# Relative-value picks as transposes in the PSUM ring, and VectorE's lower-part subtraction behind its casts

## The reference

```python
scores = jnp.einsum('bhld,bhrd->bhlr', Q, K) * scale
scores = scores + jnp.einsum('bhld,lrd->bhlr', Q, rel_k)
attn = jax.nn.softmax(scores, axis=-1)
out = jnp.einsum('bhlr,bhrd->bhld', attn, V)
out = out + jnp.einsum('bhlr,lrd->bhld', attn, rel_v)
```

## Time and profile before

| | |
|---|---|
| median of 3 runs | 3481.03 us |
| profiled execution, its own time | 3486.41 us |
| its span | 3485.2 us |
| mean granted TensorE clock | 0.951 |
| busy, share of the span | TensorE 93%, weight loads 74%, VectorE 79%, ScalarE 76%, GpSimd 63% |

### The profile page before, as it was taken

The page is one execution under the profiler, slowest core; times in us unless marked ns, Lnnn a source line. Parts: engine busy times, 40 slices in busy tenths (PEclk is TensorE's granted clock), DMA queues, the critical chain, the costliest instruction groups (busy, mean ns, idle before and its releaser), DMA issues. The chain is left out here.

```text
span 3485.2 us, 166713 instructions
## 1 busy us (share of the span) xinstructions
PE 3231.7 (93%) x65430; PEld 2576.3 (74%) x65430; DVE 2768.4 (79%) x7853; ACT 2633.0 (76%) x5852; POOL 2205.2 (63%) x2407
## 2 busy tenths in 40 slices
PE   7589999999999999999999999999999996999990
PEld 4357777777777777777777777777777785579980
DVE  6478888888888888888888888888888885534443
ACT  3288888888888888888888888888888883244440
POOL 0167777777777777777777777777777764700006
PEclk9779999999999999999999999999999997589995
DMA  6666666666666666666666666666666664712224
GB/s 211 227 228 213 220 218 221 218 221 221 215 222 220 222 221 223 221 221 223 219 219 221 222 222 219 224 219 222 218 218 223 219 212 161 236 53 66 64 61 143
DMA packets 356377, 701.33 MB, mean 201 GB/s; under 512 B 59545, under 2 KB 168706, under 8 KB 355346
## 3 DMA queue, kind: packets, MB, share of 16 engines
q1 hardware_dynamic: 349458, 673.92, 59.7%
q0 software_dynamic: 6144, 16.79, 1.5%
HBM read 343.02 MB, written 347.46 MB: 198 GB/s over the span
## 5 line engine op out<-in xcount | busy, mean ns | idle before, releaser
L851 POOL TENSOR_TENSOR pt_near<-pt_full,pt_near 128x512 f16<-128x512 f32 (+3 forms) x1984 | 1844.7, 959 | 662.9 <-DVE pt_near L1160 662.8
L1067 ACT ACTIVATE pt_full<-pb,exp_bias 128x512 f32<-128x512 f32 x2048 | 1315.1, 689 | 324.5 <-PE pb L946 240.4
L999 PEld LDWEIGHTS pb<-pt_near,table_high 128*128 128x128 f16 x18432 | 794.7, 97 | 153.4 <-issue 117.2
L999 PE MATMUL pb<-pt_near,table_high 128*128 128x64 f16 (+6 forms) x18432 | 884.7, 187 | 17.0 <-DVE rel_out L1193 16.5
L1140 DVE TENSOR_REDUCE part_max<-pb 128x1 f32<-128x512 f32 (+3 forms) x1376 | 770.5, 574 | 114.7 <-PE pb L904 114.0
L999 PE MATMUL pb<-pt_near,table_low 128*128 128x64 f16 (+6 forms) x9216 | 851.5, 187 | 0.0
L999 PEld LDWEIGHTS pb<-pt_near,table_low 128*128 128x128 f16 x9216 | 772.7, 96 | 0.1
L1136 DVE CUSTOM_DVE_ANT_0 near_sum<-pb,skewed 128x512 bf16<-128x512 f32 (+3 forms) x1216 | 675.5, 571 | 114.6 <-PE pb L904 86.2
L938 PE MATMUL pb<-ident,skewed 128*128 128x128 f32 x3840 | 625.0, 286 | 6.9 <-ACT q_max L1091 4.8
L1160 DVE CAST pt_near<-pt_full 128x512 f16<-128x512 f32 (+3 forms) x1280 | 542.4, 474 | 0.3 <-PE pb L972 0.3
L972 PE MATMUL pb<-v_head,pt_near 128*128 128x33 f16 x13440 | 501.0, 178 | 2.3 <-POOL pt_near L851 2.2
(11 more groups left out here) (183 smaller groups left out, 4087.6 us busy)
## 6 DMA issues: line engine op xcount, KB each, us to landing
skewed<-rel_scratch SPq DMA_DIRECT2D x256, 576.0 KB, 5.5
rel_scratch<-rel SPq DMA_DIRECT2D x416, 319.5 KB, 3.4
rel_scratch<-rel SPq DMA_DIRECT2D x320, 320.0 KB, 2.8
skewed<-rel_scratch SPq DMA_DIRECT2D x64, 512.0 KB, 4.5
skewed<-rel_scratch SPq DMA_DIRECT2D x64, 448.0 KB, 4.4
k_stack<-planes_scratch SPq DMA_DIRECT2D x192, 96.0 KB, 4.8
planes_scratch<-planes SPq DMA_DIRECT2D x64, 256.0 KB, 2.3
rel_scratch<-rel SPq DMA_DIRECT2D x64, 256.0 KB, 2.7
```

The costliest lines, as they stand in the source:

```text
L851: ins = nc.gpsimd.tensor_tensor(pt_piece(c, 1, a, z, near), pt_full[e][:, (a - 4 * g) * P:(z - 4 * g) * P], pt_piece(c, 0, a, z, near), AL ...
L999: ins = nc.tensor.matmul(acc[:, c0:c1, :], keep[table][:, w:w + P], pt_near[half][:, part, c0:c1, d - M_LO, a * SHIFTS:(a + 1) * SHIFTS], ...
L1067: nc.scalar.activation(pt_full[e][:, :], x_ps[e % 2][:, :], ACT.Exp, bias=exp_bias[:, 0:1]).then_inc(s_exp, 1)
```

## The change

- The picks become fp32 transposes of `rel_out` against the identity, four to a bank, in two banks of the ring (`PICK_BANKS = 2`). The ring has two more items once in eight steps, behind the maximum.
- VectorE sums the eight shifts in two reductions out of these banks into a new tile `rel_sum`, in the step in which it had made the output.
- The addition of `o_sum` and the multiplication go to GpSimd, one step later (`LAG_O = LAG_SEL + 2`), behind its lower parts of that step and ahead of the V parts. SyncE's store is issued at the third step from there instead of the eighth from the old place.
- TensorE no longer waits for the output before V products or picks.
- VectorE's lower part of group 3 is issued behind its two casts instead of ahead of them.
- The matrix `pick` and its eight mask instructions on GpSimd go, with the semaphore counts adjusted.

```diff
-LAG_O = LAG_SEL + 1
+LAG_O = LAG_SEL + 2
+PICK_BANKS = 2
+PICK_C = HALF_C // PICK_BANKS
...
-            ("scores", k - LAG_S, 1), ("scores", k - LAG_S, 3), ("max", k - LAG_A, 0)]
+            ("scores", k - LAG_S, 1), ("scores", k - LAG_S, 3), ("max", k - LAG_A, 0)] + \
+        [("pick", k - LAG_SEL, n) for n in range(PICK_BANKS) if (k - LAG_SEL) % HALF_C == 0]
...
-            for j in range(SHIFTS):
-
-                if j:
-                    pool.wait_ge(s_id, j + 2)
-                nc.gpsimd.affine_select(out=pick[:, :], in_=pick[:, :], compare_op=ALU.not_equal, fill=1.0,
-                                        base=-DK * j, pattern=[[-1, DK]], channel_multiplier=1).then_inc(s_id, 1)
...
+        rel_sum = [sb(f"rel_sum{i}", [P, HALF_C, DK]) for i in range(2)]
...
-        o_ps, s_ps = psum[6][:, 0:HALF_C * VW], psum[6][:, HALF_C * VW:HALF_C * (VW + DK)]
+        o_ps = psum[6][:, 0:HALF_C * VW]
...
+                elif last == "pick":
+                    nc.tensor.wait_ge(s_rp, PICK_BANKS * (u // HALF_C) + m + 1)
...
-                if i == HALF_C - 1 and h >= 0 and exists(it, h * HALF_C):
+                if i == 2 and h >= 0 and exists(it, h * HALF_C):
...
+            def output(it, h):
+
+                pool.wait_ge(s_rp, PICK_BANKS * (h + 1))
+                pool.wait_ge(s_or, it * HALF_STEP + h + 1)
+                if h >= 2:
+                    pool.wait_ge(s_ow[h % 2], 16 * (h // 2))
+                nc.gpsimd.tensor_tensor(out[h % 2][:, :, :], rel_sum[h % 2][:, :, :], o_sum[h % 2][:, :, :],
+                                        ALU.add).then_inc(s_o1, 1)
+                pool.wait_ge(s_o1, it * HALF_STEP + h + 1)
+                nc.gpsimd.tensor_tensor(out[h % 2][:, :, :], out[h % 2][:, :, :],
+                                        inv_sum[h % 2][:, :, :].to_broadcast([P, HALF_C, DK]), ALU.mult).then_inc(s_o, 1)
...
                     for e in range(E - 1):
                         low_part(it, u, e)
+                h, j = half_at(k, LAG_O)
+                if j == 0 and h >= 0 and exists(it, h * HALF_C):
+                    output(it, h)
...
-                    if u >= 2 * HALF_C:
-                        pe.wait_ge(s_o, it * HALF_STEP + u // HALF_C - 1)
...
-            def pick_values(it, h, i):
-
-
-                if i == 0:
+            def pick_values(it, h, n):
+
+
+                if n == 0:
 
                     pe.wait_ge(s_rle, it * (2 * HALF_STEP) + 2 * h + 2)
-                    if h:
-                        pe.wait_ge(s_o, it * HALF_STEP + h)
-                ins = nc.tensor.matmul(s_ps[:, i * DK:(i + 1) * DK],
-                                       rel_out[:, i, :, :].rearrange("p a b -> p (a b)"), keep["pick"][:, :],
-                                       start=True, stop=True)
-                if i == HALF_C - 1:
-                    ins.then_inc(s_sel, 1)
+                wait_bank(it, "pick", h * HALF_C, n)
+                for i in range(PICK_C):
+                    ins = nc.tensor.transpose(bank_of("pick", h * HALF_C, n)[:, i * P:(i + 1) * P],
+                                              rel_out[:, PICK_C * n + i, :, :].rearrange("p a b -> p (a b)"), keep["ident"][:, :])
+                ins.then_inc(s_sel, 1)
...
+            def sum_values(it, h, n):
+
+                dve.wait_ge(s_sel, PICK_BANKS * h + n + 1)
                 if h >= 2:
-                    dve.wait_ge(s_ow[h % 2], it * (16 * HALF_STEP // 2) + 16 * (h // 2))
...
+                    dve.wait_ge(s_o, it * HALF_STEP + h - 1)
+                src = bank_of("pick", h * HALF_C, n)[:, :].rearrange("p (c s d) -> p c d s", c=PICK_C, s=SHIFTS)
+                nc.vector.tensor_reduce(rel_sum[h % 2][:, PICK_C * n:PICK_C * (n + 1), :], src,
+                                        axis=AX.X, op=ALU.add).then_inc(s_rp, 1)
...
-                h, j = half_at(k, LAG_O)
+                h, j = half_at(k, LAG_SEL + 1)
                 if j == 0 and h >= 0 and exists(it, h * HALF_C):
-                    output(it, h)
+                    for n in range(PICK_BANKS):
+                        sum_values(it, h, n)
...
                     search_bank(it, a, 0)
                     search_bank(it, a, 2)
-                if exists(it, k - LAG_PV):
-                    low_part(it, k - LAG_PV, E - 1)
                 if turning:
                     high_part(it, t, 0)
                     high_part(it, t, 1)
+                if exists(it, k - LAG_PV):
+                    low_part(it, k - LAG_PV, E - 1)
```

More of the change, by code:

```diff
@@ L360, in _ @@
         def _(pool):
-            ident, pick, shift_mask = keep["ident"], keep["pick"], keep["shift_mask"]
+            ident, shift_mask = keep["ident"], keep["shift_mask"]
             nc.gpsimd.memset(keep["blank"][:, :], 0.0).then_inc(s_id, 1)
@@ L364, in _ @@
             nc.gpsimd.memset(ident[:, :], 0.0).then_inc(s_pre, 1)
-            nc.gpsimd.memset(pick[:, :], 0.0).then_inc(s_pre, 1)
             nc.gpsimd.memset(shift_mask[:, :], 1.0).then_inc(s_pre, 1)
-            pool.wait_ge(s_pre, 3)
+            pool.wait_ge(s_pre, 2)
             nc.gpsimd.affine_select(out=ident[:, :], in_=ident[:, :], compare_op=ALU.not_equal,
                                     fill=1.0, base=0, pattern=[[-1, P]], channel_multiplier=1).then_inc(s_id, 1)
-            for j in range(SHIFTS):
-                if j:
-                    pool.wait_ge(s_id, j + 2)
-                nc.gpsimd.affine_select(out=pick[:, :], in_=pick[:, :], compare_op=ALU.not_equal, fill=1.0,
-                                        base=-DK * j, pattern=[[-1, DK]], channel_multiplier=1).then_inc(s_id, 1)
             nc.gpsimd.affine_select(out=shift_mask[:, :], in_=shift_mask[:, :], compare_op=ALU.is_ge, fill=0.0,
                                     base=-DK * (SHIFTS - 1), pattern=[[DK, SHIFTS]], channel_multiplier=1).then_inc(s_id, 1)
-            pool.wait_ge(s_id, SHIFTS + 3)
+            pool.wait_ge(s_id, 3)
             nc.gpsimd.affine_select(out=shift_mask[:, :], in_=shift_mask[:, :], compare_op=ALU.is_ge, fill=0.0,
@@ L499, in _ @@
         def _(pe):
-            pe.wait_ge(s_id, SHIFTS + 4)
+            pe.wait_ge(s_id, 4)
             pe.wait_ge(s_w, 16 * weights)
@@ L620, in attend @@
         s_rle = sem("b_rel_values_on_chip")
-        s_sel = sem("b_rel_values_picked")
+        s_sel = sem("b_rel_values_turned")
+        s_rp = sem("b_rel_values_summed")
         s_o1 = sem("b_out_steps")
@@ L1044, in step @@
                 if h >= 0 and j == 0 and exists(it, h * HALF_C):
-                    for i in range(HALF_C):
-                        pick_values(it, h, i)
+                    for n in range(PICK_BANKS):
+                        pick_values(it, h, n)
             pipeline(pe, step)
@@ L1187, in mask_values @@
                 if part == 0 and h:
-                    dve.wait_ge(s_sel, it * HALF_STEP + h)
+                    dve.wait_ge(s_sel, PICK_BANKS * h)
                 half_a = SHIFT_GROUPS // 2
@@ L1193, in mask_values @@
                 nc.vector.tensor_tensor(dst, src, mask.to_broadcast([P, half_a, HALF_C, SHIFTS]), ALU.mult).then_inc(s_rle, 1)
-            def output(it, h):
-                dve.wait_ge(s_sel, it * HALF_STEP + h + 1)
-                dve.wait_ge(s_or, it * HALF_STEP + h + 1)
+            def sum_values(it, h, n):
+                dve.wait_ge(s_sel, PICK_BANKS * h + n + 1)
                 if h >= 2:
-                    dve.wait_ge(s_ow[h % 2], it * (16 * HALF_STEP // 2) + 16 * (h // 2))
-                nc.vector.tensor_tensor(s_ps.rearrange("p (c n) -> p c n", c=HALF_C), s_ps.rearrange("p (c n) -> p c n", c=HALF_C),
-                                        o_sum[h % 2][:, :, :], ALU.add).then_inc(s_o1, 1)
-                dve.wait_ge(s_o1, it * HALF_STEP + h + 1)
-                nc.vector.tensor_tensor(out[h % 2][:, :, :], s_ps.rearrange("p (c n) -> p c n", c=HALF_C),
-                                        inv_sum[h % 2][:, :, :].to_broadcast([P, HALF_C, DK]), ALU.mult).then_inc(s_o, 1)
+                    dve.wait_ge(s_o, it * HALF_STEP + h - 1)
+                src = bank_of("pick", h * HALF_C, n)[:, :].rearrange("p (c s d) -> p c d s", c=PICK_C, s=SHIFTS)
+                nc.vector.tensor_reduce(rel_sum[h % 2][:, PICK_C * n:PICK_C * (n + 1), :], src,
+                                        axis=AX.X, op=ALU.add).then_inc(s_rp, 1)
             nc.vector.memset(q_stack[0][:, :], 0.0).then_inc(s_pre, 1)
@@ L1840, in program @@
             keep["table_low"] = sbi("table_low", [P, TABLE_N * DK], FP16)
-            keep["pick"] = sbi("pick_dim", [P, DK])
             keep["blank"] = sbi("blank", [CLEAR, D])
```

## The result

The changed kernel takes 4141.4 us (median of 4 runs, 4135.91 to 4145.06) against 3480.79 us for the kernel before. The ratio is 1.1897, with a 95% interval of 1.1879 to 1.1914: 660 us slower. The forecast was 4089 us in a range of 3640 to 4270, with 0.92 on slower.

A forecast was written before the change was run, and what follows sets the result against it. TensorE, busy 2147.35 of 2200 us, was taken as the bound. Profiled 3486 - 42 (picks) + 630 (lateness) + 20 (value parts) = 4094 us; the median of runs is 5.4 lower, 4089, range 3640 to 4270.

The forecast's parts named there:

- the lateness and the value parts: TensorE reading VectorE's lower part late, 630 us over 32 heads, plus 20 us for contention from GpSimd's value parts.
- TensorE's read of the lower part as the place that decides: TensorE's V-product loads (L972) would wait on VectorE's lower part, some 600 us in all.
- The distance of 2.35 us: From the lower part's old start to TensorE's read: 0.56 + 1.16 + 0.54 + 0.09 us, with GpSimd's subtraction going first.
- The split steps: Three of 16 steps with VectorE's lower part in two instructions: readable after about 3.45 us, 2.05 late each.
- The 1.5 us a head taken back: TensorE's present waits for VectorE, 38.6 us in 26 heads, would be subtracted from the lateness.
- Order without contention: Rival, chance 0.20: VectorE keeps its turn behind the casts, lateness is casts' time less cover; 3615 to 3730 us.
- The clock: Rival, chance 0.10: TensorE's waits drop its clock to 1.2 GHz, each spell costing up to 1.3 us; 4215 to 4420.
- the forecast's own case: VectorE's lower part delayed behind casts and GpSimd's subtraction, TensorE late, full clock: 3940 to 4230 us, chance 0.62.
- the rival's mild form: Three half-clock spells of TensorE per head, adding 125 us, to 4215; part of the clock rival's 0.10.
- The picks' term of 42 us: On TensorE, eight transposes (1.29 us) replace 16 pick records (1.94 us): 0.65 us less for each of 64 halves.
- GpSimd takes the two 128x128 operations in its idle 528.6 us: Output operations moved to GpSimd, 0.442 us each, 57 us in all, would fit its waiting time.
- The prediction's terms above 4089: Upper bounds: transposes at 2.27 us each half, 63; VectorE's sums uncovered, 50; value-part contention at 60, 40 more.

The follow-up runs named there:

- the picks alone: Changed kernel with VectorE's lower part put back ahead of its casts, keeping the transposes, sums and GpSimd output: 3465.48 us.
- the order without the meeting with GpSimd: Changed kernel, but GpSimd's first subtraction of a unit waits until VectorE's lower part of the unit before is done: 3606.07 us.
- the meeting with the clock kept up: Changed kernel (the filled kernel) with ten matmuls into unused columns ahead of TensorE's wait for the last lower part: 4037.58 us.
- the order alone: Kernel before with only VectorE's lower part moved behind its casts, old picks kept: 4321.14 us.

## Why the prediction was right, and where it was not

**The whole.** The 660 us come apart along four runs: the picks alone 3465.5 (17 less), the order without the meeting with GpSimd 3606.1 (141 more), the meeting with the clock kept up 4037.6 (431 more), and the half-clock spells 4141.4 (104 more). These are differences in this sequence; another sequence would divide the interplay otherwise. The second holds the cost of GpSimd's added wait and of its own 58 us of spells.

**Partly luck.** The forecast of 4089 missed by 52 us, but three parts of it were off, together by more than that. It put 650 us for the lateness and the value parts; picks alone to the filled kernel is 572, 78 less. It put a gain of 42 for the picks and output, which is 25 too much by the run with them alone. And it put nothing for the clock, which took 104. The errors of 78 one way and of 129 the other leave the 51.

**TensorE's read of the lower part as the place that decides** was right. It waits there 612.7 us; the forecast said some 600. The other signs came too: 128x512 lower parts at 1.45 to 1.55 us (about 1.6 expected), a mean step of 6.60 us (near 6.5), and a wait of GpSimd for the casts that grew.

**The distance of 2.35 us** from where the lower part used to start was 2.37 in the step shown. The split steps were put at 3.45 and took 3.40. By step, TensorE waits 1.80 us for the lower part in the three split ones, where 2.05 was put, and 1.06 in the other thirteen, where 1.16 was put before the part taken back. That makes 19.1 a head against 21.2, 66 us over the program, which would account for most of the 78. That GpSimd's first operation, once waiting, goes first is shown from both sides: with it held back the lower part is at 683 ns, and with the lower part between the casts it is the second cast that pays.

**The 1.5 us a head taken back** from TensorE's present waits for VectorE did go. Ahead of the relative values (L999 before, now L1011) 0.8 us of waiting for VectorE are left in the whole execution, where the stretch of the earlier trace rows alone had 13.6, and in that stretch TensorE's waits of 14.7 and 10.3 us for the searches have no row at all.

**Order without contention**, the rival with 0.20, was priced at 3615 to 3730; the kernel that shows it alone took 3606.1. Its low end was 9 us too high.

**The clock** was set down as a rival with 0.10, but it was not a rival: it came in addition. What failed is the step that let the forecast's own case keep the full clock. 91 spells of about 3.5 us in 32 heads are 2.8 a head, and the filled run prices them at 104 us; the rival's mild form had three per head and 125 us. That all of it lies in the steps with a spell is shown by the comparison step by step. What TensorE did before the clock fell, here, was to wait in step after step for the lower part. By the Trainium skill (TensorE: Matmul & The Clock Gate, Part 4: PE-mode transpose) the new transposes should have made it worse; the run with the old picks in the same order had more spells (131, 621 us), so nothing here bears that out. Nor is it a clean test, since the old picks also make their steps longer.

**The picks' term of 42 us** was mis-sized on both sides. A transpose costs TensorE 0.134 us of busy time where 0.161 was put, and so the gross gain is 55 us. L938 was not the same case, as the prediction took it to be: its transposes mostly come in groups of three to five, the new ones eight at a time. From start to start the median is 0.109 us for both; the whole 0.28 us of the last one of a group is what makes the mean differ. The 275 ns of the Trainium skill (TensorE: Matmul & The Clock Gate, Part 4: PE-mode transpose) is close to the duration here, 277 ns, but as the price of one in a row it was further off than 0.161. The other step that failed is "GpSimd takes the two 128x128 operations in its idle 528.6 us": the idle time isn't in the steps where the output stands. The picks alone gave 17 us.

**The range's upper end.** The prediction's terms above 4089, 63 + 50 + 40, add up to 4242 and not 4230. Nothing hangs on it.

**20 us for the value parts** was not measured by itself in the changed kernel.

**What stays open.** Why the old picks go with more and longer spells than the transposes in the same order. Of the transposes' 55 us some 48 show in their two steps in the run with the picks alone, and 27 once the output is moved; why the output's place costs step 5 and step 13 what it does was only tested by moving it once more, and the two steps answered differently.

## What to carry to other kernels

Before an operation is moved behind another, ask who reads it and how long before its reader comes it is done today; here that gap was under 0.8 us in every step, and the move cost more. Then ask what will run beside it in the new place: here two engines held each other off, a lower part took 1.65 us instead of 0.69 behind an operation of GpSimd, and an added wait was worth far more than it cost. An engine's idle time as a sum says little about a new task; the step in which it is put does. And a total that comes out near the forecast still has to be taken apart: here three terms were off and partly cancelled.

## What was not expected of the hardware

The filler: 5120 matmuls whose results nobody reads made the kernel 104 us faster, by keeping TensorE's granted clock at 1.00 instead of 0.95 between 700 and 2700 us; on the order alone it was 204 us (0.91 to 0.99). The kernel before, with 2.4% of TensorE's time idle, never lost it in its attention part; with 1.25 us idle in steps of 6.6 us (busy 1620.77 of 2000 us) it was lost 91 times. And fp32 transposes start 0.109 us apart, though each lasts 0.28 us: eight in a row are busy for 0.134 us each, groups of three to five for 0.161.
